# Two-block adaptive attention and feed-forward kernel: transposed queries moved by DMA, another order of the iteration, opening rebuilt

## The chip, the core and the metric

The kernel runs on one core of a Trainium2 chip. A core has TensorE (PE in the profile), VectorE (DVE), ScalarE (ACT), GpSimd (POOL) and SyncE (SP), each with its own instruction queue, which is worked off in order; the engines meet only through semaphores. DMAs are issued from the queue of SP or of ACT. The metric is device time in microseconds (us), the median of the runs.

## The reference

Sixteen sequences of 256 tokens and 256 features. What matters here is the first half, the attention block; the second half (a conditional feed-forward layer "cond2" and a gated feed-forward network "ffn" of width 1024) is not touched by the change.

```python
def _L0_cond_ref(hidden_states, language_ids, W1, b1, W2, b2, gamma, beta):
    w1, w2 = W1[language_ids], W2[language_ids]
    h = relu(einsum('bsh,bha->bsa', hidden_states, w1) + b1[language_ids][:, None, :])
    x = hidden_states + einsum('bsa,bah->bsh', h, w2) + b2[language_ids][:, None, :]
    normed = (x - mean(x)) * rsqrt(var(x) + 1e-5)
    return normed * gamma[language_ids][:, None, :] + beta[language_ids][:, None, :]

def _L0_attn_ref(x, segment_pos, Wq, Wk, Wv, Wf, bf):      # 16 heads of 16, one key and one value head
    q = (x @ Wq.T).reshape(b, t, 16, 16); k = x @ Wk.T; v = x @ Wv.T
    logits = einsum('btnh,bsh->bnts', q, k) * 16 ** -0.5    # causal mask
    probs = softmax(where(mask, logits, -1e30))
    return einsum('bnts,bsh->btnh', probs, v).reshape(b, t, 256) @ Wf.T + bf

x = x + _L0_attn_ref(_L0_cond_ref(x, ...), ...)
x = x + _L0_ffn_ref(_L0_cond2_ref(x, ...), ...)
```

## The kernel before

The attention block is a software pipeline over the 16 sequences. One call of `iteration(b, ...)` on each engine holds four strands at once: the **front** of sequence b + 2 (adapter, layer norm, projections), the **maxima** of sequence b + 1 (all scores, and on DVE their row maxima, in 12 units), the **softmax** of sequence b (scores again with the maximum folded in as extra rows of the product, and exponentials on ACT, in 12 units), and the **tail** of sequence b - 1 (products with the values, division, output projection). Iterations -1 and 0 open the pipeline, B - 2 = 14 and B - 1 = 15 close it, the 13 between them (1 to 13) hold all four strands. There is no scheduler: on each engine the order of the work is the order in which `iteration` calls its helpers.

Scores are computed in float32r (one pass), and keep float32 accuracy by stacking: a column of `q_t` (128 partitions, two heads of 64 rows) has 16 rows of the high part of a query, 16 rows of its low part, 16 rows of the high part again, and two rows for the maximum; `keys` has the matching rows. In the kernel before, the queries are projected with tokens on partitions (`project_queries`, L1200, two halves of 272 columns, with the values in the last 16), DVE splits them into high and low parts in `q_parts` (`queries_of`, L881 to L885), POOL copies the high part once more (`high_again`, L484), PE transposes `q_parts` in 16 blocks of 128x128 per sequence (`queries_transposed`, L1216), and ACT copies the four banks to `q_t` (`queries_out`, L609). Keys are split on DVE (`keys_of`, L869 to L872) and spread over the two heads' row blocks by POOL (`move_keys`, L494); values are copied by POOL (`move_values`, L502). `q_t`, `keys` and `values` have two buffers each.

The maxima are transposed on PE (`maxima_transposed`, L1242), copied by ACT (`maxima_out`, L634) into `m_t`, and moved into the maximum rows of `q_t` by four DMAs of 8 KB on SP's queue (`move_maxima`, L309). The first score product of that sequence waits for them (`scores`, u = 0, L1253). SP's queue holds in each iteration: the front loads of sequence b + 3 (`load_front`, five DMAs), `store_x1`, `load_resid`, then `move_maxima`.

After the pipeline come the cond2 phase (from the end of iteration 15) and the ffn phase, both bound by PE. The weights of the ffn phase are combined by POOL (`combine`), stored to DRAM by a DMA of 1792 KB on ACT's queue (`finish_chunk`, L682) and scanned by ACT (L687); the first such store is issued at the end of iteration 14, between `move_maxima`'s wait and its DMAs.

## Time and profile before

| | us |
|---|---|
| median of 3 runs | 1155.56 (1155.26 to 1156.74) |
| the profiled execution, its own time | 1157.74 |
| its span, first to last instruction | 1156.0 |
| opening, to the first maxima transpose | 42.55 |
| iteration 0 | 18.97 |
| iterations 1 to 13 | 282.37 (steady ones 21.56 each) |
| iteration 14 | 19.12 |
| to the first product with the values of sequence 15 | 20.20 |
| cond2 and ffn phases | 772.79 |

PE is busy 97% of the span, DVE 70%, ACT 51%, POOL 19%. A busy PE in the profile includes the modelled ends of pipelined matmuls, so the cost of a group of matmuls is read from its start to the start of the next group. The stages are cut at the starts of L1242, one per sequence.

### The profile page before, as it was taken

What the parts mean: (1) busy time and instruction counts of PE and PEld (TensorE: products, weight loads), DVE (VectorE), ACT (ScalarE), POOL (GpSimd) and SP (SyncE); (2) the same over time, 40 slices, a digit from 0 to 9 for tenths busy, and PEclk for the clock granted to TensorE, in tenths of its full rate; (3) what the DMA queues carried; (4) which work ended last, traced back from release to release, by engine and by line L of the source; (5) the groups of instructions that cost most, each with busy time, mean ns of one, the idle gap of its engine ahead of it and who ended that gap; (6) DMA issues with size and microseconds to landing.
All of it is one profiled execution on the core that took longest, in us unless ns stands there. A gap on an engine that the chain in (4) does not pass through costs nothing.

```text
span 1156.0 us, 18793 instructions
## 1 busy us (share of the span) xinstructions
PE 1117.5 (97%) x6148; PEld 892.6 (77%) x6178; DVE 804.4 (70%) x1440; ACT 594.7 (51%) x989; POOL 214.6 (19%) x266
## 2 busy tenths in 40 slices
PE   4899999999998999999999999999999999999998
PEld 3567777777775788888888888888888888888886
DVE  2877777776776557756577875778656887568875
ACT  1355655555555634533365654556445565455653
POOL 2233333343345444452000000000000000000000
PEclk9999999999999999999999999999999999999999
DMA  4342122122143456654515443044440444304420
GB/s 122 111 149 60 53 59 63 48 60 63 47 160 124 151 187 202 227 188 150 204 35 164 140 167 115 10 164 146 162 137 0 163 146 163 137 8 145 145 91 37
DMA packets 66765, 135.97 MB, mean 118 GB/s; under 512 B 13793, under 2 KB 28017, under 8 KB 66545
## 3 DMA queue, kind: packets, MB, share of 16 engines
q1 hardware_dynamic: 57696, 114.49, 30.5%
q10 hardware_dynamic: 9024, 20.97, 5.0%
q8 instruction: 18, 0.29, 0.1%
q14 instruction: 27, 0.21, 0.1%
HBM read 107.65 MB, written 30.41 MB: 119 GB/s over the span
## 4 chain that ended last, share of the span: by engine, by line
PE 89%; DVE 6%; SPq 2%; issue 1%; DMA 1%; ACT 1%; POOL 0%; DVEq 0%; POOLq 0%; ACTq 0%
PE bank L1531 35%; PE bank L1493 10%; PE bank L1319 7%; PE bank L1543 5%; PE bank L1469 4%; PE bank L1463 4%; PE bank L1253 4%; PE bank L1234 3%; DVE neg_max L891 2%; PE bank L1274 2%; PE bank L1311 2%; PE bank L1216 2%; PE bank L1200 2%; PE bank L1237 1%; PE bank L1189 1%
## 5 line engine op out<-in xcount | busy, mean ns | idle before, releaser
L1531 PE MATMUL bank<-op_lo,w_ring 128*128 128x512 f32 x896 | 348.6, 389 | 0.0
L1531 PE MATMUL bank<-op_hi,w_ring 128*128 128x512 f32 x896 | 348.6, 389 | 0.0
L1066 DVE TENSOR_TENSOR op_lo<-x_blk,op_hi 128x512 fp32r<-128x512 f32 x288 | 193.8, 684 | 30.4 <-ACT op_hi L764 30.3
L764 ACT ACTIVATE op_hi<-x_blk 128x512 fp32r<-128x512 f32 x288 | 162.8, 620 | 73.6 <-PE bank L1531 69.3
L1531 PEld LDWEIGHTS bank<-op_lo,w_ring 128*128 128x128 f32 x896 | 168.2, 188 | 34.9
L1531 PEld LDWEIGHTS bank<-op_hi,w_ring 128*128 128x128 f32 x896 | 168.2, 188 | 34.9
L891 DVE TENSOR_REDUCE neg_max<-bank 128x2 f32<-128x512 f32 (+1 forms) x192 | 126.0, 685 | 48.0 <-remote 39.7
L617 ACT ACTIVATE p<-bank 128x512 f32<-128x512 f32 x192 | 111.3, 599 | 71.9 <-PE bank L1253 68.2
L788 ACT ACTIVATE x_blk<-x_blk,scales 128x512 f32<-128x512 f32 x96 | 69.3, 722 | 67.0 <-DVE x_blk L1119 28.9
L1493 PE MATMUL bank<-tile_hi,ffn_w 128*128 128x512 f32 x256 | 101.5, 396 | 0.0
L1493 PE MATMUL bank<-tile_lo,ffn_w 128*128 128x512 f32 x256 | 101.5, 396 | 0.0
L1253 PE MATMUL bank<-q_t,keys 128*128 128x512 f32 x192 | 95.5, 515 | 4.8 <-DMA q_t<-m_t 4.2
L1234 PE MATMUL bank<-keys,q_t 128*128 128x256 f32 (+1 forms) x256 | 86.0, 392 | 7.5 <-DVE neg_max L891 6.4
L717 ACT ACTIVATE g_raw<-bank,fc_bias 128x512 f32<-128x512 f32 x64 | 44.0, 689 | 92.2 <-PE bank L1319 77.9
L511 POOL TENSOR_SCALAR_AFFINE_SELECT p<-p 128x512 f32<-128x512 f32 (+1 forms) x96 | 75.8, 789 | 66.8 <-ACT p L617 66.8
L776 ACT ACTIVATE sil<-bank,scales 128x512 f32<-128x512 f32 x64 | 44.0, 689 | 79.7 <-PE bank L1493 79.7
L1074 DVE SCALAR_TENSOR_TENSOR x_blk<-bank,scales,sil 128x512 f32<-128x512 f32 x64 | 48.1, 751 | 52.4 <-PE bank L1493 50.2
L1234 PEld LDWEIGHTS bank<-keys,q_t 128*128 128x128 f32 x256 | 48.1, 191 | 20.2 <-DVE neg_max L891 10.7
L562 POOL TENSOR_TENSOR comb<-comb 128x512 f32<-128x512 f32 x32 | 49.5, 1547 | 56.5 <-DVE g_parts L1032 55.0
L1493 PEld LDWEIGHTS bank<-tile_hi,ffn_w 128*128 128x128 f32 x256 | 48.2, 188 | 11.7
L1493 PEld LDWEIGHTS bank<-tile_lo,ffn_w 128*128 128x128 f32 x256 | 48.2, 188 | 11.7
L1032 DVE TENSOR_TENSOR g_parts<-g_raw,g_parts 128x512 fp32r<-128x512 f32 x64 | 52.1, 814 | 2.2
(124 smaller groups left out, 1850.0 us busy)
## 6 DMA issues: line engine op xcount, KB each, us to landing
w_ring<-hid_scratch SPq DMA_DIRECT2D x112, 512.0 KB, 4.6
hid_scratch<-comb ACTq DMA_DIRECT2D x8, 1792.0 KB, 7.6
comb<-in_hid_d ACTq DMA_DIRECT2D x6, 768.0 KB, 5.1
xt<-in_x_t SPq DMA_DIRECT2D x16, 256.0 KB
xtok<-in_x_tok SPq DMA_DIRECT2D x16, 256.0 KB
resid<-in_x_t SPq DMA_DIRECT2D x16, 256.0 KB, 3.1
x_scratch<-x SPq DMA_DIRECT2D x16, 256.0 KB, 2.6
tile_in<-x_scratch SPq DMA_DIRECT2D x8, 512.0 KB, 4.1
```

Source lines behind the costliest of these rows:

```text
L511: nc.gpsimd.affine_select(out=v, in_=v, compare_op=ALU.is_ge, fill=0.0, base=0, pattern=[[0, v.shape[1]], [1, P]], channel_multiplier=-1). ...
L617: nc.scalar.activation(dst.rearrange("p c t -> p (c t)"), score_bank[par][:, :], ACT.Exp).then_inc(s["exp_done"], 1)
L764: nc.scalar.activation(op_hi[:, o % OP_RING, k], x_blk[:, operand_home(o), k], ACT.Copy).then_inc(s["op_hi"], 1)
L788: nc.scalar.activation(x_blk[:, at[block], m], src, ACT.Gelu, scale=sc[:, KB * row + m:KB * row + m + 1]).then_inc(s[made], 1)
L891: nc.vector.tensor_reduce(neg_max[:, t, first:first + pairs, :].rearrange("p c a -> p (c a)"), max_bank[u % 2][:, :].rearrange("p (c k) -> ...
L1066: nc.vector.tensor_tensor(op_lo[:, o % OP_RING, k], x_blk[:, operand_home(o), k], op_hi[:, o % OP_RING, k].bitcast(F32), ALU.subtract).the ...
L1234: mm(dst[:, 2 * c * seen:2 * (c + 1) * seen].rearrange("p (a k) -> p a k", a=2), q_t[odd][:, first + c, t * P:(t + 1) * P], keys[odd][:, : ...
L1253: mm(score_bank[par][:, :].rearrange("p (c t) -> p c t", c=pairs), keys[odd][:, par, k0:k0 + P], q_t[odd][:, first:first + pairs, q0:T], s ...
L1319: last = mm(bank, w[:, k, cols], v[:, k, :], start=i == 0, stop=i == len(passes) - 1)
L1493: last = mm(bank, w_at(at, k, HID, m), read(v[:, half, k, :]), start=k == 0 and v is yc_hi, stop=k == KD - 1 and v is yc_lo)
L1531: last = mm(banks[first_bank + m][:, :], w, read(v[:, q % OP_RING, k, :]), start=k == 0 and v is op_hi and i not in (P2, P3), stop=k == KB ...
L1543: last = mm(banks[4 + 2 * half + m][:, :], w_at(W3_AT, k, D, m), read(v[:, o % OP_RING, n % KB, :]), start=n == 0 and v is op_hi, stop=n = ...
```

## The change

- **Queries transposed by the projection.** `wqv` and `wk` become `wq` and `wkv`. `project_queries` now computes with the weights as the stationary operand, so that the result comes out with features on partitions and tokens on columns, in one bank; the columns of `wq` are ordered so that partition hd * 8 + pair holds one row of a head. ACT takes the high part (`queries_high`), DVE the low one (`queries_low`). The rows are then brought into `q_t` by six DMAs of 128 KB per sequence: four for the two copies of the high part, on ACT's queue (`move_high`), two for the low part on SP's queue (`move_queries`). `queries_transposed`, `queries_out`, `queries_of` and `high_again` are gone.
- **Keys and values** are projected together. ACT copies the bank to `kv` (`keys_copied`) and writes both row blocks of `keys` (`keys_high`), DVE subtracts for the low rows (`keys_low`), PE transposes `kv` in two blocks (`values_transposed`), DVE copies the values out (`values_of`). `move_keys` and `move_values` on POOL are gone.
- **Three buffers** (`SLOTS = 3`) for `q_t`, `keys` and `values`; the hardware loop holds three iterations.
- **Another order** of the helpers in `iteration` on PE, DVE, ACT, POOL, and of SP's queue: rest of the loads, front loads, `move_queries`, `move_maxima`, then `store_x1`, `load_resid`.
- **Opening**: the loads of sequence 0's adapter weights go on ACT's queue, beside those on SP's; nine matmuls on zeros (`keep_warm`) and a dummy activation (`warm_row`) run before the data is there; iteration -1 has an order of its own: the whole front of sequence 1, then the maxima of sequence 0.
- **End**: `finish_chunk` is cut into `store_chunk` and `check_chunk`; the first store waits until the last maxima have been moved.

The core of the diff:

```diff
+SLOTS = 3
+            def move_queries(n, slot):
+                sp.wait_ge(s["q_low"], n + 1)
+                settle(sp, "sp_settled")
+                for par in range(2):
+                    row = SLOT * par + HD
+                    sp.dma_start(q_t[slot][row:row + HD, :, :].bitcast(F32), q_rest[:, par, :].bitcast(F32)).then_inc(s["q_moved"], 16)
...
-                    load_front(b + 3)
+                    load_rest(b + 3, l)
+                    load_inputs(b + 3, l)
+                    move_queries(b + 2, (step + 2) % SLOTS)
+                    move_maxima(b + 1, (step + 1) % SLOTS)
                     store_x1(b - 1)
                     load_resid(b)
-                    move_maxima(b + 1, 1 - step % 2)
...
+            def queries_high(n):
+                act.wait_ge(s["q_mm"], n + 1)
+                if not is_first(n):
+                    act.wait_ge(s["q_moved"], 96 * n)
+                nc.scalar.activation(q_high[:, :, :], ring[0][:, :].rearrange("p (a t) -> p a t", a=2), ACT.Copy, scale=QSCALE).then_inc(s["q_hi"], 1)
+            def move_high(n, slot):
+                act.wait_ge(s["q_hi"], n + 1)
+                for i in (0, 2):
+                    for par in range(2):
+                        row = SLOT * par + HD * i
+                        act.dma_start(q_t[slot][row:row + HD, :, :].bitcast(F32), q_high[:, par, :].bitcast(F32)).then_inc(s["q_moved"], 16)
+            def keys_copied(n):
+                act.wait_ge(s["kv_mm"], n + 1)
...
+                nc.scalar.activation(kv[:, :], ring[1][:, 0:T], ACT.Copy).then_inc(s["kv_out"], 1)
+            def keys_high(n, slot):
+                act.wait_ge(s["kv_out"], n + 1)
+                for par in range(2):
+                    nc.scalar.activation(keys[slot][:, par, :], kv[:, :], ACT.Identity,
+                                         bias=key_row[:, 2 * par:2 * par + 1], scale=key_row[:, 2 * par + 1:2 * par + 2]).then_inc(s["keys_hi"], 1)
...
+            def project_queries(n, tail):
+                pe.wait_ge(s["norm_t_out"], n + 1)
...
+                for m in range(KD):
+                    for k in range(KD):
+                        last = mm(ring[0][:, m * T:(m + 1) * T], wq[:, k, m * P:(m + 1) * P], norm_t[:, k, :], start=k == 0, stop=k == KD - 1)
+                last.then_inc(s["q_mm"], 1)
...
+            def values_transposed(n):
+                pe.wait_ge(s["kv_out"], n + 1)
+                for t in range(NT):
+                    last = nc.tensor.transpose(ring[1][:, T + t * P:T + (t + 1) * P], kv[:, t * P:(t + 1) * P], ident[:, :])
+                last.then_inc(s["v_t_mm"], 1)
...
             def max_scores(n, slot, u):
...
                 if u == 0:
-                    pe.wait_ge(s["keys_moved"], 2 * (n + 1))
-                    pe.wait_ge(s["qv_out"], NT * (n + 1))
+                    pe.wait_ge(s["q_moved"], 96 * (n + 1))
+                    pe.wait_ge(s["keys_out"], 2 * (n + 1))
...
+                if softmax and not maxima:
+                    act.wait_ge(s["maxima_moved"], 64 * B)
+                    store_chunk(0)
...
+            nc.vector.memset(warm, 0.0).then_inc(s["warm_made"], 1)
+            pe.wait_ge(s["warm_made"], 1)
+            keep_warm(WARM_LOADS)
```

PE at the end of a full iteration and the beginning of the next. Before (`bank<-wqv,norm_t` is the projection of queries and values, `bank<-ident,m` the transpose of the maxima, `bank<-ident,q_parts` that of the queries, `bank<-xt,w1c` the first matmul of the next front):

```order
L1200 MATMUL bank<-wqv,norm_t 128x272 x2
L1311 MATMUL bank<-att_t,wf 128x256 x4
L1250 REGISTER_ALU
L1253 MATMUL bank<-q_t,keys 128x512
L1250 REGISTER_ALU
L1253 MATMUL bank<-q_t,keys 128x512
L1242 MATMUL bank<-ident,m 32x128 x2
L1197 REGISTER_ALU
L1200 MATMUL bank<-wqv,norm_t 128x272 x2
L1206 REGISTER_ALU
L1216 MATMUL bank<-ident,q_parts 128x128 x8
```

And now (`bank<-ident,kv` is the transpose of the values):

```order
L1365 MATMUL bank<-att_t,wf 128x256 x4
L1307 REGISTER_ALU
L1310 MATMUL bank<-q_t,keys 128x512
L1307 REGISTER_ALU
L1310 MATMUL bank<-q_t,keys 128x512
L1299 MATMUL bank<-ident,m 32x128 x2
L1273 MATMUL bank<-ident,kv 128x128 x2
L1307 REGISTER_ALU
L1310 MATMUL bank<-q_t,keys 128x512
L1221 ISA
L1225 REGISTER_ALU
L1227 MATMUL bank<-xt,w1c 128x256 x2
```

The transposes of the queries and the second half of their projection have left this place; the last score product of the sequence now stands behind the transpose of the values, as PE's last work ahead of the next front. The projection of the queries itself now stands earlier, ahead of four maximum units and the projection of the keys.

ACT in the second half of a full iteration. Before (`p<-bank` is an exponential, `att_t<-bank` the transposed attention, `m_t<-bank` the maxima, `q_t<-bank` the transposed queries):

```order
L602 ACTIVATE norm_t<-bank,vec 128x256 x2
L628 ACTIVATE att_t<-bank 128x512
L613 REGISTER_ALU
L617 ACTIVATE p<-bank 128x512
L613 REGISTER_ALU
L617 ACTIVATE p<-bank 128x512
L613 REGISTER_ALU
L617 ACTIVATE p<-bank 128x512
L613 REGISTER_ALU
L617 ACTIVATE p<-bank 128x512
L631 REGISTER_ALU
L633 REGISTER_ALU
```

And now:

```order
L631 ACTIVATE p<-bank 128x512
L603 ISA
L604 ACTIVATE q_high<-bank 128x512
L612 DMA q_t<-q_high 16x8x256 x4
L617 REGISTER_ALU
L618 ACTIVATE kv<-bank 128x256
L623 ACTIVATE keys<-kv,key_row 128x256 x2
L627 REGISTER_ALU
L631 ACTIVATE p<-bank 128x512
L647 ISA
L648 ACTIVATE m_t<-bank 32x256
```

Between the exponentials 8 and 9 of a sequence stand now the high parts, four DMA issues, the copy of keys and values and the two writes of `keys`.

## Rows read from the trace of the kernel before

**Rows 1.** Busy time by stage: us, then each engine's busy time; PEclk is the granted clock
```profile
0.00:42.55 42.55, 23.90 (x88) 16.54 (x89) 20.04 (x47) 6.43 (x11) 7.09 (x17) 0.96 0.39 115
61.52:343.89 282.37, 275.53 (x2132) 205.21 (x2159) 205.81 (x481) 156.62 (x298) 107.65 (x159) 1.00 0.25 76
343.89:363.01 19.12, 17.73 (x145) 12.69 (x146) 14.04 (x28) 10.96 (x21) 13.26 (x16) 1.00 0.24 72
363.01:383.21 20.20, 16.02 (x111) 10.59 (x109) 9.08 (x13) 11.58 (x19) 8.04 (x8) 0.83 0.44 146
```
**Rows 2.** Timeline of PE, one steady iteration: start us, us, engine, line, what
```profile
192.85 1.04 PE L1216 MATMUL bank<-ident,q_parts 128*128 128x128 f32 x8
193.72 1.03 PE L1166 MATMUL bank<-xt,w1c 128*128 128x256 f32 x4
...
196.48 0.64 PE L1274 MATMUL bank<-p,values 128*32 128x256 f32 x8
...
199.22 0.50 PE L1253 MATMUL bank<-q_t,keys 128*128 128x512 f32 x1
...
208.31 1.03 PE L1189 MATMUL bank<-norm_t,wk 128*128 128x256 f32 x4
208.99 0.58 PE L1253 MATMUL bank<-q_t,keys 128*128 128x512 f32 x1
209.41 0.40 PE L1234 MATMUL bank<-keys,q_t 128*128 128x512 f32 x1
...
210.13 1.08 PE L1200 MATMUL bank<-wqv,norm_t 128*128 128x272 f32 x4
211.05 1.94 PE L1311 MATMUL bank<-att_t,wf 128*128 128x256 f32 x8
212.63 0.82 PE L1253 MATMUL bank<-q_t,keys 128*128 128x512 f32 x2
213.29 0.38 PE L1242 MATMUL bank<-ident,m 128*32 128x128 f32 x2
213.51 1.08 PE L1200 MATMUL bank<-wqv,norm_t 128*128 128x272 f32 x4
```
**Rows 3.** Timeline of ACT, the same iteration
```profile
199.85 2.39 ACT L617 ACTIVATE p<-bank 128x512 f32<-128x512 f32 x4
...
207.12 1.02 ACT L602 ACTIVATE norm_t<-bank,vec 128x256 f32<-128x256 f32 x2 [1.07 <-PE bank L1183]
...
214.22 0.36 ACT L634 ACTIVATE m_t<-bank 32x256 fp32r<-32x256 f32 x1
```
**Rows 4.** Timeline of SP's queue, the same iteration: the issues of the maxima's DMAs
```profile
194.33 2.87 SPq L309 DMA_DIRECT2D q_t<-m_t  x4
```
**Rows 5.** The tile `m_t`: ns min/median/max of one issue
```profile
L309 SPq DMA_DIRECT2D q_t<-m_t x64: 625/660/1374, 43.4 to 369.4; - x64
```
**Rows 6.** Timeline of ACT's queue: one issue of the store of the combined weights
```profile
398.60 0.38 ACTq L682 DMA_DIRECT2D hid_scratch<-comb  x1
```
**Rows 7.** The chain that ended last, iterations 14 and 15: start us, us, what
```profile
349.01 1.94 DMA q_t<-m_t
351.00 0.50 PE bank L1253
...
369.41 3.17 DMA q_t<-m_t
372.63 0.51 PE bank L1253
```
**Rows 8.** DMA issues of the page: queue, count, KB each, us from issue to landing
```profile
resid<-in_x_t SPq DMA_DIRECT2D x16, 256.0 KB, 3.1
```
**Rows 9.** Timeline of the opening
```profile
7.96 2.05 PE L1166 MATMUL bank<-xt,w1c 128*128 128x256 f32 x4 [7.96 <-DMA vec<-in_cond_vec]
...
10.09 1.28 ACT L597 ACT_TABLE_LOAD   x1 [10.09 <-PE bank L1166]
...
48.53 0.50 PE L1253 MATMUL bank<-q_t,keys 128*128 128x512 f32 x1 [0.67 <-DMA q_t<-m_t]
```

More of the change, by code:

```diff
@@ L207, in build @@
         ident = sb("ident", [P, P], F32, one)
-        values = [sb(f"values{i}", [P, NT, 32], F32, one) for i in range(2)]
+        values = [sb(f"values{i}", [P, NT, 32], F32, one) for i in range(SLOTS)]
         pv = sb("pv", [P, 4, T], F32, one)
@@ L939, in iteration @@
                 if maxima:
+                    maximum(b + 1, 0)
+                    maximum(b + 1, 1)
+                if front:
+                    normalise(b + 2)
+                if maxima:
                     maximum(b + 1, 2)
-                    maximum(b + 1, 3)
                 if tail:
@@ L949, in iteration @@
                     maximum(b + 1, 5)
+                    maximum(b + 1, 6)
+                    maximum(b + 1, 7)
+                    maximum(b + 1, 8)
+                    maximum(b + 1, 9)
                 if front:
[L951 to L956 removed]
+                    queries_low(b + 2)
                 if maxima:
```

541 lines of the change are left out of this document (282 added, 259 removed).

## The prediction

> **What bounds the kernel now.** I read the busy time by stage first. In the thirteen full iterations PE is busy 275.53 of 282.37 us, an idle time of 6.84 us or 0.53 per iteration, with the clock at its full level, while DVE is busy 73%, ACT 55% and POOL 38% [rows 1]. So PE sets the pace there, and work that leaves PE is time, as long as nothing else comes late in its place. Next the timeline of PE over one steady iteration, from one transpose of the maxima (L1242) to the next: 21.56 us; the mean of the thirteen is 21.72, the first and the last being longer [rows 1, 2]. Then ACT and SP's queue for the same stretch, because the change gives ACT new duties [rows 3, 4]. Last, the ends: between 363.01 and 383.21 the granted clock is 0.83 on average and PE is idle for 4.2 us [rows 1], and the chain there runs through the maxima's DMA, 3.17 us, where iteration 14 had 1.94 [rows 7].
>
> **PE's own work.** Taken from start to start. Removed: two groups of eight query transposes. The one shown lasts from 192.85 to 193.72, 0.87, so 1.74 for both. The projection of the queries was two groups of 0.92 (210.13 to 211.05); its new shape, four matmuls of 256 columns by two blocks, is that of the output projection, 1.58 (211.05 to 212.63), so 0.26 less. Added: two transposes of the values, priced like the two of the maxima, 0.22 (213.29 to 213.51) [rows 2]. Sum -1.74 - 0.26 + 0.22 = -1.78. Without any idle time the iteration would be 21.56 - 1.78 - 0.53 = 19.25. Waits shorter than the modelled tail of a matmul don't show as idle, so up to half a us more may go: floor 18.7 to 19.25.
>
> **ACT's four DMA issues.** This is the term that costs. After the projection of the queries ends (call it T) ACT must do, in order: the high parts, 0.13 after T and 0.60 long like an exponential (2.39 / 4); four issues; the copy of keys and values, 0.36 as for the maxima; two writes of `keys`, 1.02 as for the two of L602; exponential 9, 0.60 [rows 3]. The issue of an SBUF-to-SBUF DMA whose two sides cut the rows differently is in the trace only on SP, four in 2.87 [rows 4], median 0.66, from 0.63 to 1.37 each [rows 5]; the nearest on ACT's own queue is a store, 0.38 [rows 6]. I take 2.87, since shape and spaces are the same. With 0.05 for each of three semaphores: 0.13 + 0.60 + 2.87 + 0.36 + 1.02 + 0.60 + 0.15 = 5.73, plus the last score product, which waits for exponential 9, 0.33: the next iteration can start at T + 6.06. PE's own way there is four maximum units of 0.36 (209.41 to 210.13 holds two), the keys 0.68, the output projection 1.58, three score products of 0.33 (212.63 to 213.29 holds two) and two transposes of 0.22 [rows 2]: 5.13. So ACT is late by 0.93, and PE waits that long ahead of its last score product. Floor plus 0.93 gives 19.6 to 20.2; I take **19.8** per iteration: 13 x 19.8 = 257.4 against 282.37, **-25.0 us**.
>
> **What could be late next.** The queries: the last high part's issue starts at T + 2.95, and with 1.94 [rows 7] to 3.1 us [rows 8] to land they are there by T + 6.1. PE needs them at the first maximum unit, some 4.7 us into the next iteration (T + 10.8): 4.7 us to spare. The low parts, issued from SP after one DVE operation, are no later. The maxima: ACT copies them behind exponential 9, until T + 6.1; three issues of 0.72 and 1.94 for the last bring T + 10.3. PE reaches the first score product 5.50 after the start of the front (193.72 to 199.22 [rows 2]), less one maximum unit that is now behind it, so at T + 11.1: 0.8 to spare. SP no longer puts a store and a load ahead of these DMAs. The front's loads are issued by T, 6 us before they are wanted. DVE loses two passes of the query split and POOL the copies; neither was bound.
>
> **Opening.** For it: the adapter's weights come from a second queue, three issues earlier (about 1.5 us); the table load, 1.28, leaves the path; the warm-up matmuls let the first adapter matmuls run at the full clock: the first group takes 2.05 for what costs 1.03 later [rows 2, 9], so about 1 us each for two groups. Together the norm of sequence 0 is some 4.9 us earlier. Against it: twice, for sequences 0 and 1, ACT's four issues (2.87) and the copy stand ahead of the values' transpose, and on PE that transpose stands ahead of the next adapter matmul and of the third maximum unit; behind it ten maximum units follow, each paced by DVE, where before the maxima began ahead of the front's middle. I get the first score product, 48.53 before [rows 9], at 50.3, and lose little more in iteration 0: **+1.5 us**, between -4 and +5, as the clock stays up or not. The Trainium skill, TensorE: Matmul & The Clock Gate, Part 1, says that the half rate is the default, that activity releases it and that idleness brings it back. By that rule the gap between the adapter and the norm can undo the warm-up, the worse half of this range; the trace agrees that the first group ran at half the speed of the later ones.
>
> **The end.** In iteration 14 the first score product came 7.1 us after the transpose of the maxima (343.89 to 351.00 [rows 1, 7]); now 0.93 + 0.36 + 4.1 = 5.8 at most, -1.3, and eight transposes go, -0.9. In iteration 15 the store of 1792 KB no longer runs beside the last maxima, and a store and a load no longer precede them on SP: the wait of about 3 us goes (369.41 to 372.63 [rows 7]). Without it the clock should not fall (0.83 in this stage, 1.00 in its neighbours [rows 1]), and from the first score product to the products with the values, 10.6 us (372.63 to 383.21), should take about twelve exponentials and one copy, 8: -2.6. Together **-8 us**, between -9.5 and -5. The phases behind have no edit that reaches them.
>
> **Sum.** -25.0 + 1.5 - 8.0 = -31.5. The profiled execution took 1157.74 (span 1156.0), which becomes 1126.2; it lay 2.2 above the median of the runs, so on the median, 1155.56, I forecast **1124.0 us**. Its own range: 19.2 to 20.4 per iteration with the ends' bounds, 1113 to 1135.
>
> **Rivals.**
> - *Cheap issues.* If ACT issues as on its own store, 0.38 each [rows 6], ACT's way is 1.35 shorter, less than PE's 5.13, and PE waits for nothing: 19.0 per iteration, -35.4; the opening gains 2.7 of the same: -44.6, **1111 us**. For: it is ACT's own queue. Against: the shape is another. 0.14.
> - *More hand-offs than I counted.* The iteration becomes shorter than its chains DVE-PE-ACT allow here and there, each wait short: 20.8, -12.0, with the ends -18.5: **1137 us**. The 0.53 of idle time with a longer iteration speaks for some. 0.12.
> - *Late queries.* All six transfers write 16 partitions each. The data part of 256 KB over 128 partitions is 3.1 - 1.94 = 1.16, so 0.58 for 128 KB. Were each four times as slow and the four one after another, 9.3, they would land at T + 12.1, 1.3 too late: 21.1 per iteration, -8.1, and the opening 3 worse: -11.6, **1144 us**. The Trainium skill, SBUF — State Buffer, section "Door 1: The DMA port swizzle", says that DMA bandwidth depends on how many of the 16 ports the partitions reach, and by its formula 16 neighbouring partitions reach four; no row of this case shows that. 0.10.
> - *Slower: dear issues.* If one issue on ACT takes what the slowest on SP took, 1.37 [rows 5], ACT is 2.6 us later still in each iteration: 22.4, +8.9, the opening 5.2 worse, the end as above: +7.6, **1163 us**. It decides from 31.5 / 60 = 0.53 above 0.72, so from 1.25 us per issue (52 issues in the loop, 8 in the opening). For: 16 rows to 128 partitions is more than the 8 KB on SP. Against: the median of 0.66. 0.09.
> - *It comes to nothing*, two of these in part: within 0.2% of before, 0.03.
>
> **How the numbers follow.** Likeliest 0.52 (1124), cheap issues 0.14, hand-offs 0.12, late queries 0.10: faster 0.88. Same 0.03. Slower 0.09. The bound of 0.2% (2.3 us) is about what a measurement of this kernel can tell from no change. The range takes in all but the last two and the outer parts of the first two: 1106 to 1146.
>
> **What would show it.** In the profile after: no idle time of PE but one near 0.9 us ahead of the last score product of each sequence, ended by ACT's exponential; ACT's queue with four issues in 2.9; the period between transposes of the maxima 19.8; the clock at 1.00 through iteration 15 and no wait there for `q_t<-m_t`; the first score product near 50. If ACT's issues take over 1.2 us, or PE's first maximum unit waits for the moved queries, the forecast is wrong; if PE's idle time has gone and the period is 19 or less, ACT was cheaper than I took it.

## The result, and the profile after

The changed kernel takes **1161.16 us** (median of 20 runs, 1157.3 to 1167.22) beside 1156.67 for the kernel before (20 runs, 1155.26 to 1161.41): ratio 1.003, 95% interval 1.0018 to 1.0041. It is slower by a little, where 1124.0 was forecast. (Here and below the ratio and its interval are the recorded estimate; the quotient of the two medians printed beside it can differ by up to 0.002.) Its profiled execution has a span of 1160.3 us, 4.3 above that of before.

The steady loop did become shorter, and about as much as forecast. Nearly all of it was given back elsewhere. The first view to read is therefore the busy time by stage, with the cuts at the transposes of the maxima as in [rows 1]. The columns are the stretch, its length, the busy time of PE, PE's weight loads, DVE, ACT and POOL with their instruction counts, the granted clock, the DMA engines' busy share and GB/s. Of the changed kernel:

```profile
0.00:56.24 56.24, 33.66 (x88) 20.12 (x89) 19.82 (x46) 8.62 (x16) 7.67 (x18) 0.80 0.47 102
56.24:75.20 18.96, 17.24 (x64) 11.64 (x66) 13.11 (x25) 7.68 (x15) 3.77 (x5) 0.77 0.23 58
75.20:96.00 20.80, 19.76 (x152) 14.42 (x154) 13.91 (x32) 12.56 (x25) 5.54 (x7) 1.00 0.91 275
96.00:126.23 30.23, 21.48 (x152) 15.23 (x152) 14.88 (x34) 12.02 (x25) 5.44 (x7) 0.83 0.47 101
126.23:348.33 222.10, 216.28 (x1663) 158.34 (x1673) 163.31 (x364) 130.98 (x252) 62.59 (x79) 1.00 0.52 113
348.33:370.47 22.14, 18.23 (x128) 11.78 (x128) 14.43 (x27) 10.16 (x20) 9.86 (x9) 0.85 0.40 83
370.47:388.47 18.00, 14.68 (x112) 9.29 (x111) 10.90 (x14) 12.69 (x20) 9.92 (x10) 1.00 0.48 163
```

And of the kernel before, two stages that [rows 1] holds only within its steady stretch (iterations 1 and 2):

```profile
61.52:83.63 22.11, 21.47 (x165) 15.75 (x167) 15.46 (x37) 11.19 (x22) 8.16 (x13) 1.00 0.53 175
83.63:105.50 21.87, 21.22 (x166) 15.79 (x167) 15.80 (x38) 12.21 (x24) 8.13 (x13) 1.00 0.20 57
```

| stage | before | after | difference |
|---|---|---|---|
| opening, to the first transpose of the maxima | 42.55 | 56.24 | +13.7 |
| iteration 0 | 18.97 | 18.96 | 0.0 |
| iteration 1 | 22.11 | 20.80 | -1.3 |
| iteration 2 | 21.87 | 30.23 | +8.4 |
| iterations 3 to 13 | 238.39 | 222.10 | -16.3 |
| iteration 14 | 19.12 | 22.14 | +3.0 |
| iteration 15, to its first product with the values | 20.20 | 18.00 | -2.2 |
| all behind it | 772.8 | 771.8 | -1.0 |
| span | 1156.0 | 1160.3 | +4.3 |

Each column is one execution. Where experiments below leave a stage's code as it is, their executions show how much it moves by itself: the changed kernel's opening took 56.24 here and 55.33 in e5, its iteration 1 20.80 here and 22.34 and 22.41 in e3 and e5, its iteration 2 between 24.2 and 30.2 (e5, e3, e4, e2). The eleven iterations stay within 0.15 us (e1, e2, e5, e8), but for e3 with 223.48, and the part behind within 0.05.

**The steady iteration.** PE of the changed kernel, from the query projection to the next iteration, to be laid beside [rows 2] (start us, us, engine, line, what, and in brackets an idle time and what ended it):

```profile
200.82 1.89 PE L1257 MATMUL bank<-norm_t,wq 128*128 128x256 f32 x8
...
207.10 0.38 PE L1299 MATMUL bank<-ident,m 128*32 128x128 f32 x2
...
208.18 0.50 PE L1310 MATMUL bank<-q_t,keys 128*128 128x512 f32 x1 [0.48 <-ACT p L631]
```

and ACT for the same stretch, beside [rows 3]:

```profile
202.83 0.60 ACT L604 ACTIVATE q_high<-bank 128x512 fp32r<-128x512 f32 x1 [1.08 <-PE bank L1257]
203.46 2.55 ACTq L612 DMA_DIRECT2D q_t<-q_high  x4
206.13 0.38 ACT L618 ACTIVATE kv<-bank 128x256 f32<-128x256 f32 x1 [2.70 <-issue]
206.55 1.09 ACT L623 ACTIVATE keys<-kv,key_row 128x256 fp32r<-128x256 f32 x2
207.55 0.57 ACT L631 ACTIVATE p<-bank 128x512 f32<-128x512 f32 x1
```

The chain is there in the order forecast: high parts, four issues in 2.55 us, the copy of keys and values held up behind them for 2.70, the two writes of `keys`, the exponential, and PE waiting 0.48 for it. The period is 20.05 us, with every third at 20.46; the mean of the eleven is 222.10 / 11 = 20.19, against 238.39 / 11 = 21.67. Of the 16.3 us, 1.3 are iteration 13: before waits 1.31 there for DVE's norm, at 337.08, and takes 22.82 for it where its other ones take 21.56.

**The opening.** PE's timeline of the changed kernel:

```profile
1.53 4.02 PE L1490 MATMUL bank<-att 128*128 128x512 bf16 x9 [1.53 <-DVE att L1058]
9.05 2.04 PE L1227 MATMUL bank<-xt,w1c 128*128 128x256 f32 x4 [3.50 <-DMA vec<-in_cond_vec]
...
17.68 1.09 PE L1246 MATMUL bank<-ident,norm 128*128 128x128 f32 x4 [3.89 <-DVE norm L908]
...
27.53 0.69 PE L1273 MATMUL bank<-ident,kv 128*128 128x128 f32 x2 [2.75 <-ACT kv L618]
28.01 1.91 PE L1227 MATMUL bank<-xt,w1c 128*128 128x256 f32 x4
...
36.28 1.12 PE L1246 MATMUL bank<-ident,norm 128*128 128x128 f32 x4 [3.72 <-DVE norm L908]
38.51 3.78 PE L1257 MATMUL bank<-norm_t,wq 128*128 128x256 f32 x8 [1.11 <-ACT norm_t L596]
41.73 1.87 PE L1291 MATMUL bank<-keys,q_t 128*128 128x256 f32 x4
```

and the same places of the kernel before:

```profile
17.89 1.09 PE L1183 MATMUL bank<-ident,norm 128*128 128x128 f32 x4 [3.91 <-DVE norm L859]
...
27.83 0.58 PE L1234 MATMUL bank<-keys,q_t 128*128 128x256 f32 x2
```

Up to 28 us the kernels are level: the norm of sequence 0 is transposed at 17.68 and 17.89. Then before starts its maximum units at 27.83, and runs the front of sequence 1 between them. The changed kernel runs sequence 1's front alone, with nothing to fill its gaps, and starts its maximum units at 41.73: 13.9 us later, which is the whole of the +13.7. One window over it shows the price twice, in idle time and in the clock (0.50 is the lower of the two levels, 1.2 GHz):

```profile
28.00:41.73 13.73, 8.34 (x23) 5.51 (x21) 5.60 (x14) 2.09 (x5) 0.70 (x1) 0.50 0.45 77
```

**Iteration 2.** One wait on PE, and SP's queue ahead of it:

```profile
105.85 2.07 PE L1227 MATMUL bank<-xt,w1c 128*128 128x256 f32 x4 [8.29 <-DMA w2c<-in_cond_w]
```
```profile
80.02 0.44 SPq L413 DMA_DIRECT2D comb<-in_hid_d  x1
...
82.79 0.60 SPq L337 DMA_DIRECT2D ffn_scratch<-in_ffn_d  x1
...
91.25 0.58 SPq L294 DMA_DIRECT2D w1c<-in_cond_w  x1
92.02 0.47 SPq L295 DMA_DIRECT2D w2c<-in_cond_w  x1
```

`w2c` is 65 KB. PE is ready for it at 97.56, 5.5 us after its issue, and gets it at 105.85, 13.8 us after. Ahead of it are 2 MB of combining loads and the ffn store (3 MB, the size of the load that reads it back), issued from 80.02 to 83.39. Iteration 1, in which they start, has a DMA share of 0.91, where the eleven iterations behind have 0.52. In the kernel before, the loads and the store stand apart: SP issues the four loads from 38.65 to 40.50, in the opening, and the store at 65.29:

```profile
65.29 0.60 SPq L317 DMA_DIRECT2D ffn_scratch<-in_ffn_d  x1
```

The change moved only the four loads, from the opening to directly ahead of the store. The store stands behind `move_maxima(1, 1)` in both kernels, and by itself there it made PE wait for no front load in iteration 2 of the kernel before, where iteration 1 had a DMA share of 0.53.

**Iteration 14.** What PE waits for, and POOL's queue, in which the causal mask (L520) stands behind a combining step (L561):

```profile
350.84 0.49 PE L1310 MATMUL bank<-q_t,keys 128*128 128x512 f32 x1 [1.17 <-ACT p L631]
...
355.46 1.08 PE L1329 MATMUL bank<-p,values 128*32 128x256 f32 x8 [1.81 <-POOL p L520]
```
```profile
351.68 1.70 POOL L561 TENSOR_TENSOR comb<-comb 128x512 f32<-128x512 f32 x1
353.33 2.07 POOL L520 TENSOR_SCALAR_AFFINE_SELECT p<-p 128x1024 f32<-128x1024 f32 x1
```

### The profile page after: what moved, and what is told of

The parts are those of the page before. It is cut to its first block, busy times and chain, and to the rows that moved or that the text cites. A ratio compares the mean times of both kernels' runs of the same rounds, so it can differ in the third digit from the quotient of the medians.

```text
span 1160.3 us, 17988 instructions
## 1 busy us (share of the span) xinstructions
PE 1108.4 (96%) x5947; PEld 876.8 (76%) x5963; DVE 788.9 (68%) x1377; ACT 593.1 (51%) x990; POOL 175.8 (15%) x192
## 4 chain that ended last, share of the span: by engine, by line
PE 87%; ACTq 4%; ACT 3%; issue 2%; DVE 2%; DMA 2%; POOL 1%; SPq 0%; DVEq 0%; POOLq 0%
PE bank L1605 35%; PE bank L1567 10%; PE bank L1373 7%; PE bank L1617 5%; PE bank L1543 4%; PE bank L1537 4%; PE bank L1310 4%; ACTq L612 3%; PE bank L1291 3%; PE bank L1329 3%; PE bank L1257 3%; PE bank L1237 2%; PE bank L1227 2%; PE bank L1294 2%; DMA w2c<-in_cond_w 1%
## 5 line engine op out<-in xcount | busy, mean ns | idle before, releaser
L631 ACT ACTIVATE p<-bank 128x512 f32<-128x512 f32 x192 | 110.2, 593 | 29.5 <-PE bank L1310 23.8
L520 POOL TENSOR_SCALAR_AFFINE_SELECT p<-p 128x512 f32<-128x512 f32 (+1 forms) x96 | 77.7, 810 | 168.8 <-ACT p L631 168.7
L1310 PE MATMUL bank<-q_t,keys 128*128 128x512 f32 x192 | 89.4, 506 | 9.1 <-ACT p L631 9.0
L1291 PE MATMUL bank<-keys,q_t 128*128 128x256 f32 (+1 forms) x256 | 92.3, 415 | 2.2 <-DVE neg_max L935 2.1
L561 POOL TENSOR_TENSOR comb<-comb 128x512 f32<-128x512 f32 x32 | 50.2, 1567 | 56.5 <-DVE g_parts L1093 55.0
L1294 PE MATMUL bank<-mask,ident_b 128*128 128x256 bf16 (+1 forms) x176 | 56.3, 320 | 0.0
```

The costliest lines, as they stand in the source:

```text
L520: nc.gpsimd.affine_select(out=v, in_=v, compare_op=ALU.is_ge, fill=0.0, base=0, pattern=[[0, v.shape[1]], [1, P]], channel_multiplier=-1). ...
L631: nc.scalar.activation(dst.rearrange("p c t -> p (c t)"), score_bank[par][:, :], ACT.Exp).then_inc(s["exp_done"], 1)
L1291: mm(dst[:, 2 * c * seen:2 * (c + 1) * seen].rearrange("p (a k) -> p a k", a=2), q_t[slot][:, first + c, t * P:(t + 1) * P], keys[slot][:, ...
L1294: mm(diag, ident_b[:, :], mask[:, 0:2 * pairs, :], start=False, stop=True).then_inc(s["max_mm"], 1)
L1310: mm(score_bank[par][:, :].rearrange("p (c t) -> p c t", c=pairs), keys[slot][:, par, k0:k0 + P], q_t[slot][:, first:first + pairs, q0:T], ...
```

## The experiments

Each was timed beside the kernel before on the same chip, in one of three groups: before took 1158.14 us for e1 to e4, 1157.8 for e5 to e8, 1157.7 for e9 and e10. Across groups the ratios are compared; the changed kernel's is 1.003. In the diffs a minus is a line of the kernel named, a plus one of the experiment. Stage lengths come from each one's profiled execution.

**e1, the bulk transfers in the opening.** The four loads go back to the place that they have in the kernel before, and the store goes into the opening as well, where before doesn't have it. (The later expectations call both "as before" or "at their old place"; that is right of the loads alone.) On the changed kernel:

```diff
             move_queries(0, 0)
+            store_ffn()
             load_front(2)
+            (the four loads of comb[0], comb[1])
             sp.wait_ge(s["const_made"], 3)
...
             move_maxima(1, 1)
-            (the four loads of comb[0], comb[1])
-            store_ffn()
```

> The changed kernel with one thing moved on SP's queue: the 3 MB copy of the ffn weights and the 2 MB of loads for the combining are issued in the opening, behind the first sequence's query moves, and no longer at 80 us, ahead of iteration 2's loads. Theory 1 (these transfers hold up the front loads of iteration 2, on which PE waits 8.3 us): the stage from the third to the fourth transpose of the maxima falls from 30.2 to about 20.3, and the whole by 8 to 10 us against the changed kernel, ratio to before 0.996. Rival (the moved queries' own traffic, 768 KB per sequence, is what delays the loads): the wait stays or moves to another iteration, and the whole stays within 2 us of the changed kernel.

Measured: 1152.31 us, ratio 0.9934 (0.9909 to 0.9959). Iteration 2 takes 20.08 instead of 30.23, with no DMA wait of PE, while the opening stays at 56.20:

```profile
97.47:117.55 20.08, 19.61 (x152) 14.40 (x152) 14.88 (x34) 12.03 (x25) 5.45 (x7) 1.00 0.51 98
```

Iteration 1 takes 22.39 where it took 20.80, so the two together fall by 8.6, from 51.03 to 42.47. So the 8.4 us that iteration 2 had over before are the doing of where the 5 MB are issued. The edit moves both parts; a run with the loads alone at their old place wasn't made.

**e2, the opening in the order of the other iterations.** On the changed kernel, in ACT's, DVE's and PE's `iteration`:

```diff
-                if not softmax:
-                    (an order of its own for the opening's iteration -1)
-                    return
```

> The changed kernel without the special order of iteration -1: it runs in the order of the other iterations, with the maximum units of sequence 0 between the steps of sequence 1's front. Theory 1 (the opening is long because twelve maximum units and their DVE steps stand behind the whole front of sequence 1): the first transpose of the maxima comes at 46 to 48 us and no longer at 56.2, the whole falls by 8 to 10 us. Rival (the opening is long because TensorE runs at half its clock and ACT issues four DMAs ahead of the keys, whatever the order): the first transpose stays above 54.

Measured: 1152.14 us, ratio 0.9948 (0.9929 to 0.9966). The opening takes 45.84 instead of 56.24, and iteration 2 keeps its wait (7.64 for `w2c`, 29.97 us long):

```profile
0.00:45.84 45.84, 29.61 (x86) 17.86 (x88) 18.63 (x41) 7.79 (x15) 7.68 (x18) 0.89 0.48 116
```

Of the opening's 13.7 us, 10.4 are this order. The other 3.3 are not taken apart. In this execution the first maximum unit starts at 32.37, where before has 27.83; ahead of it PE waits 2.27 us for ACT's copy of keys and values, which stands behind the four issues, and 1.07 us for `q_t<-q_high`. There is also a granted clock of 0.89 where before has 0.96 [rows 1]. Another wait, 2.31 for `q_t<-q_rest` at 51.32, falls into iteration 0.

**e3, no warm-up.** `WARM_LOADS, WARM_NORM = 9, 14` becomes `0, 14`: the nine matmuls on zeros ahead of the first adapter product are left out.

> The changed kernel without the nine warm-up matmuls. In its trace the first adapter group took 2.04 us after them, as long as 2.05 before, so theory 1 says they buy nothing: the whole within 1 us of the changed kernel, first transpose of the maxima at 56. Rival (they shorten the opening by letting the later groups reach the full clock): 2 us or more slower than the changed kernel.

Measured: 1161.47 us, ratio 1.0025 (1.0011 to 1.0038), which is the changed kernel's. The opening takes 54.55 where it took 56.24: the warm-up gains nothing here. The first adapter product takes 2.04 behind it, as the 2.05 without a warm-up in [rows 9]; in the loop it takes 1.03 [rows 2].

Three other executions with the same warm-up show what became of it. In e5 the granted clock is 1.00 from 5.20 to 8.60 and 0.50 from 8.60 to 25.60; in e7 it falls at 8.4, in e1 at 9.1. So there the clock did rise, just as the nine matmuls ended (in e5 the ninth took 0.51 us where the eight others took 0.61 to 0.63), and it had fallen again when the first product started, at 8.76, 9.42 and 9.51, since PE had nothing to do until the adapter's data landed. In the changed kernel's execution, in e3's and in the others the clock's record only begins between 23.8 and 24.7 us. Ahead of its first entry the views print 1.00, also where products take 2.04; so the 0.80 of the opening in the first view is too high.

**e4, all transfers of queries issued by SyncE.** They are six a sequence, four high and two low (the later expectations' "eight" is a slip). On the changed kernel:

```diff
-            (ACT) move_high(n, slot): wait for q_hi, four dma_start of q_high
             (SP) move_queries(n, slot):
+                sp.wait_ge(s["q_hi"], n + 1)
+                (four dma_start of q_high)
                 sp.wait_ge(s["q_low"], n + 1)
```

> The changed kernel with all six moves of the queries issued from SP's queue, none from ACT's. Theory 1 (the four issues, 2.5 us, keep ACT from the exponential on which PE's last score product waits): ACT's gap ahead of the copy of the keys goes, PE's wait of 0.45 ahead of the last score product goes, the steady period falls from 20.05 to 19.5 or less, the whole by 5 to 8 us against the changed kernel; the opening gets shorter by some 2 us twice. Rival (two queues are needed, six issues in a row on one queue land too late for the first maximum unit, or delay the maxima's own DMAs): PE waits at the first maximum unit or the first score product, the whole the same or slower.

Measured: 1147.26 us, ratio 0.99 (0.9881 to 0.9919), 1.3% below the changed kernel.

```profile
0.00:52.66 52.66, 31.39 (x89) 18.72 (x90) 19.74 (x46) 8.62 (x16) 7.68 (x18) 0.87 0.49 109
121.60:338.87 217.27, 216.46 (x1663) 158.38 (x1673) 163.38 (x364) 133.82 (x254) 62.09 (x79) 1.00 0.55 116
338.87:356.52 17.65, 15.69 (x129) 10.73 (x129) 15.13 (x27) 8.77 (x17) 8.69 (x9) 1.00 0.49 100
```

The eleven iterations take 217.27 instead of 222.10, and PE is idle for 0.8 us of them instead of 5.8: ACT's issues cost 4.83 / 11 = 0.44 per iteration, the wait of 0.48. They cost another 3.6 in this order of the opening (2.7 against the 55.33 of e5) and 4.5 in iteration 14, where the clock now stays up. The whole gained 13.9 us where 5 to 8 had been expected: the expectation had no term for iteration 14. The transfers land as fast from SP, 4.0 us against 4.1 for the high parts in the loop: no wait for `q_t` there.

**e5, the masks first.** On the changed kernel, in POOL's `iteration`:

```diff
+                if softmax:
+                    causal(b, 5)
                 if last_front:
                     combine(0, 2)
                 elif last_maxima:
                     combine(1, 1)
-                if softmax:
-                    causal(b, 5)
```

> The changed kernel, with one step of GpSimd's order moved: the last causal mask of an iteration stands ahead of the combining of the scores, which only iterations 14 and 15 have. Theory 1: iteration 14 of the changed kernel takes 22.1 us where before took 19.1, and 1.8 of the 3 us are TensorE's wait for that last mask, which stands behind a combine of 1.7 us; the same wait in iteration 15 is 1.5 us. Then iteration 14 takes 20.3 to 20.8, the wait of the value products for the mask is gone from both, and the whole is 2 to 3.5 us shorter than the changed kernel (about 1158.5 to 1159). Rival: ScalarE, with its four issues, sets iteration 14; the value products then wait as long for the exponentials instead of the mask, iteration 14 stays at 22 and the whole at 1161.

Measured: 1155.76 us, ratio 0.9983 (0.9967 to 0.9999): 0.5% below the changed kernel. Iteration 14 is 18.32 us long, a gain of 3.8 where the wait aimed at was 1.81, and the clock is at its full level where it was 0.85; the wait of 1.17 for the exponential is still there. Iteration 15 gives 1.0 more (17.00 to its first product with the values), the wait of 1.52 for its last mask being gone:

```profile
342.89:361.21 18.32, 15.87 (x129) 10.68 (x128) 14.32 (x27) 10.00 (x20) 9.45 (x9) 1.00 0.45 97
```

e4 left the mask behind the combine, with 1.52 of wait for it, and had 17.65 all the same. So the +3.0 needed both: the exponentials late behind ACT's issues, and the mask behind a combine. Either edit alone takes it away. In this profiled execution, the fastest of its ten, iteration 2 also took 24.21, with 2.31 of wait for `w2c` instead of 8.29. The code at that place is the same in five kernels, and the waits are 8.29 (changed kernel), 7.64 (e2), 7.23 (e4), 2.50 (e3) and 2.31 (e5): the size of this loss varies from execution to execution, and 8.4 is one draw of it. The store lands at 99.6 in the changed kernel's execution and at 95.9 and 96.0 in e3's and e5's.

**e6, the kernel before with its first store of combined weights late.** On the kernel before, ACT's part for the last iterations:

```diff
+                if softmax and not maxima:
+                    act.wait_ge(s["maxima_moved"], 64 * B)
+                    store_chunk(0)
                 if softmax:
                     for u in range(0, 4):
...
                 if maxima and not front:
-                    finish_chunk(0)
+                    check_chunk(0)
```

(`finish_chunk` is parted into its store and the rest. The expectation gives that store 256 KB; the page has it at 1792.)

> The kernel before, with one part of the change's end: the first store of combined scores (256 KB) is issued by ScalarE after the last maxima have been moved, not ahead of them. Theory 1: that store was in the way of the transfers of sequence 14's and 15's maxima, for which TensorE waited 1.94 and 3.17 us; with the store out of the way iterations 14 and 15 lose 3 to 5 us, and the whole comes to 1152 to 1154 where before is 1156.7. Rival: those waits were the transfers' own time at that place and not the store's doing; the waits stay above 1.5 us each and the whole stays within 1 us of before.

Measured: 1152.81 us, ratio 0.9953 (0.9933 to 0.9973). From the last transpose of the maxima to the first product with sequence 15's values it takes 15.09 where before took 20.20, and the score product waits for no DMA but 0.46 for ACT:

```profile
362.40:377.49 15.09, 13.57 (x112) 8.96 (x110) 9.03 (x13) 11.61 (x19) 8.05 (x8) 1.00 0.60 194
```
```profile
370.16 0.98 PE L1260 MATMUL bank<-q_t,keys 128*128 128x512 f32 x2 [0.46 <-ACT p L617]
```

The 5.1 us of this stage are the 5.0 of the median. Iteration 14 stays as it was, 19.11 with its own wait for `q_t<-m_t`; the expectation's 1.94 there is the transfer's landing time in the chain, of which PE was idle for 0.48 only.

**e8, e1 and e2 together.**

> The changed kernel with the store of the ffn and the first combining loads back at their old place, and no order of its own for the opening's first iteration; ScalarE keeps its four issues. Theory 1: the two alone gave -8.9 and -9.0 us against the changed kernel, in stages that don't meet: together 1143 (1141 to 1146), the opening at 46 and iteration 2 at 20. Rival: the early stores and loads run into the transfers of an opening that is 10 us shorter: iteration 2 or the opening keeps 4 us or more, and the whole is 1147 to 1152. The difference between this kernel and the one with all transfers on SyncE's queue is what ScalarE's four issues cost over the whole kernel: 13 to 14 us by theory 1.

Measured: 1148.07 us, ratio 0.9903 (0.9876 to 0.9929). The rival's number holds: the two don't add up. The place is another than it named: the opening is 45.78 and iteration 2 20.06, but now iteration 0 takes 26.11, with a wait of 8.36 for `q_t<-q_rest` at 57.31. In e1 alone the same burst had an opening 10 us longer to pass in; that this is why it hurt nobody there is argued, not shown.

**e7, e8 with e4 and e5 as well.**

> The changed kernel with four parts set otherwise at once: all eight transfers of transposed queries issued by SyncE, none by ScalarE; the store of the ffn and the first combining loads issued ahead of the front's loads, as before; no order of its own for the opening's first iteration; the last mask ahead of the combine. Theory 1: the three costs are in different stages (opening -10, iteration 2 -8 to -9, ScalarE's issues -14 with iteration 14 among them) and add up: opening 43 to 46 us, iteration 2 at 19.7, later iterations at 19.6, the whole near 1129 (1126 to 1133), 2.4% below before. Rival: they meet in one queue. With eight issues of 0.7 us a sequence on SyncE behind it, the combining loads and the stores collide with the moved loads, and iteration 2 keeps 3 us or more of its wait; or the opening, where SyncE now has all the work, gives back less than 5 us: the whole is then above 1136.

Measured: 1137.43 us, ratio 0.9808 (0.9783 to 0.9834), above the 1136 at which the rival was to hold. The parts that the rival named gave back what they should (opening 46.77, iteration 2 20.52); the loss is in iteration 0, 26.46 us long. Against e8 it is 10.6 us faster, where 13 to 14 were expected for ACT's issues, and 3.6 of these are iteration 14, which e7's mask accounts for in part. In the opening the issues cost nothing here: 46.77 without them on ACT, 45.78 with them in e8. Two waits for moved queries, one in the opening and one in iteration 0:

```profile
33.35 0.79 PE L1258 MATMUL bank<-keys,q_t 128*128 128x256 f32 x2 [4.23 <-DMA q_t<-q_rest]
59.03 0.80 PE L1258 MATMUL bank<-keys,q_t 128*128 128x256 f32 x2 [9.09 <-DMA q_t<-q_rest]
```

SP's queue just ahead of the second: four combining loads, 2 MB, and directly behind them the moves of 128 KB on which iteration 0 depends.

```profile
41.39 0.42 SPq L414 DMA_DIRECT2D comb<-in_hid_d  x1
...
43.51 2.71 SPq L321 DMA_DIRECT2D q_t<-q_high  x4
```

The kernel before issues the same four loads at about that place (38.65), and its iteration 0 has no queries that go by DMA. With queries that do, the same place is a bad one.

**e9, e7 with the 5 MB parted.**

```diff
             (SP: the last load of the constants)
+            store_ffn()
             load_front(1)
             sp.wait_ge(s["const_made"], 1)
             move_queries(0, 0)
-            store_ffn()
             load_front(2)
-            (the loads of comb[0], comb[1])
             sp.wait_ge(s["const_made"], 3)
             move_queries(1, 1)
             move_maxima(0, 0)
+            (the loads of comb[0])
             load_front(3)
             move_queries(2, 2)
             move_maxima(1, 1)
+            (the loads of comb[1])
```

> The kernel with all eight transfers on SyncE and four parts set otherwise, once more, with the 5 MB of the ffn store and the first combining loads parted: the store (3 MB) goes out in the opening, ahead of sequence 1's front loads, and one chunk of combining loads (1 MB) behind each of the first two moves of maxima. Theory 1 (where a burst is issued decides whom it holds up): the two waits for q_t<-q_rest of that kernel, 4.2 us in the opening and 9.1 us in iteration 0, were the burst's doing, since the store was issued 1 us and the combining loads 1 to 3 us around those moves; without it iteration 0 takes 19 to 20 where it took 26.5, no w2c wait comes back in iteration 2, and the whole is 8 to 12 us shorter: 1128 (1125 to 1131). Rival: the moves of 128 KB are late for another reason, the six issues in a row on SyncE, and the waits stay in good part: the opening at 46 and iteration 0 at 24 or more, the whole above 1133.

Measured: **1131.38 us, ratio 0.976 (0.9736 to 0.9784)**, faster than both kernels. The profiled execution took 1135.31, the slowest of the four. Iteration 0 takes 19.58 instead of 26.46, iteration 2 20.17:

```profile
45.73:65.31 19.58, 15.33 (x66) 10.45 (x67) 14.14 (x29) 9.34 (x18) 3.90 (x6) 0.91 0.62 131
...
85.67:105.84 20.17, 19.62 (x152) 14.39 (x152) 14.84 (x34) 12.14 (x24) 5.42 (x7) 1.00 0.49 98
105.84:323.64 217.80, 216.38 (x1663) 158.34 (x1672) 163.28 (x364) 133.64 (x254) 61.91 (x79) 1.00 0.56 115
```

The gain over e7 is 6 us of the 8 to 12 expected; the whole is just above the range of 1125 to 1131. The wait in the opening stayed, though the store, issued at 8.23, had landed at 21.8, so it was not the burst's doing, and that part goes to the rival, the six issues in a row on SP (24.39 to 28.29, the low parts last). Two more are left in the execution shown:

```profile
32.90 0.79 PE L1259 MATMUL bank<-keys,q_t 128*128 128x256 f32 x2 [4.82 <-DMA q_t<-q_rest]
51.34 0.80 PE L1259 MATMUL bank<-keys,q_t 128*128 128x256 f32 x2 [2.44 <-DMA q_t<-q_rest]
330.98 0.80 PE L1259 MATMUL bank<-keys,q_t 128*128 128x256 f32 x2 [2.74 <-DMA q_t<-q_rest]
```

**e10, e9 with the change's two queues.** The high parts are issued by ACT again.

> The same with the changed kernel's two queues: ScalarE issues the four high moves, SyncE the low ones. Theory 1: the opening and iterations 0 to 2 as with all on SyncE or 1 to 2 us longer, the steady iteration at 20.05 to 20.15 where it is 19.6 to 19.7, iteration 14 near 18.3 (the mask is ahead of the combine): the four issues on ScalarE cost 0.45 us in each of 13 iterations and 1 to 3 us in the opening, 7 to 9 us in all: 1136 (1133 to 1139). Rival: high moves that leave earlier by another queue repay that in the opening, and the two kernels are within 4 us.

Measured: 1139.86 us, ratio 0.9844 (0.9818 to 0.9869), 8.5 us above e9 and inside the 7 to 9 us expected for the price of ACT's issues (the whole is just above its own range of 1133 to 1139):

```profile
108.56:330.92 222.36, 216.28 (x1662) 158.35 (x1672) 163.39 (x364) 131.39 (x253) 62.49 (x79) 1.00 0.52 113
```

The Trainium skill, DMA: Bandwidth & Descriptors, section "Issuing engines are not separate DMA queues", says that issuing from several engines saves only issue time on the sequencer, usually small beside the DMA. The pair agrees that the second queue makes nothing land sooner: in the eleven iterations the high parts land in 4.1 us from either engine. But the issue time is not small where the engine has work behind it, 2.55 us of ACT per sequence. SP issues as fast and computes nothing, so there it holds up only its own queue.

## Why the prediction was wrong

**The steady iteration: right in mechanism, 0.25 too short in size for the period, 0.4 for the mean.** Forecast 19.8, measured 20.05 and 20.19 in the mean. ACT's way was worked out with 2.87 for the issues where 2.55 was measured, so the wait is 0.48 and not 0.93. PE's own work fell less than forecast, from 275.53 / 13 = 21.19 to 216.28 / 11 = 19.66, by 1.53 and not 1.78, and little of the half a us of hidden short waits came free: 20.05 less the wait is 19.57, where the 19.8 had 18.87 in it. So one error made the forecast 0.45 too long and the other 0.7 too short. The turn of the hardware loop, 0.4 us in every third iteration, was in no term. For the thirteen iterations at the measured 20.19 the term would have been -19.9 instead of -25.0. "Cheap issues" and "dear issues" fall: an issue costs 0.62 in the median on ACT, beside 0.66 on SP [rows 5]. "More hand-offs" falls too: the period is not 20.8, and the one wait is where it was forecast.

**The opening: the step that failed first.** Forecast +1.5 (-4 to +5), measured +13.7. Three parts of it went wrong.
- The norm of sequence 0 was to come 4.9 us earlier (its three parts add up to 4.8) and came 0.2 earlier. The loads on the second queue landed at 9.05, later than 7.96 [rows 9]; the matmuls behind the warm-up took 2.04 still, because the higher clock, where the record shows it, was gone again by then (e3). Only the table load left the path, and DVE's part behind it didn't move: 3.89 of wait against 3.91.
- The sentence "ten maximum units follow, each paced by DVE, where before the maxima began ahead of the front's middle" named the mechanism and gave it no price. It is the price: sequence 1's front, 13.7 us on a PE with nothing in its gaps and the clock at 0.50, stood beside the maximum units before and stands ahead of them now. I had the two start times in the order of the changed instructions and never set them on a time line. e2 shows 10.4 us of it.
- The rest, 3.3, is open. In the changed order ACT's issues are 3.6 of the opening by e4; in e2's order they are not, since there the opening takes 45.78 with them on ACT (e8) and 46.77 with all on SP (e7), and 46.98 (e10) against 45.73 (e9) with the store out of the way. The forecast had them in its +1.5, at 2.87 for each of two sequences.

**What could be late next: the transfers were priced as if alone.** "The front's loads are issued by T, 6 us before they are wanted" is right for the steady loop, where the last is issued at 203.05 and wanted at 208.85. It says nothing of iteration 2, where 5 MB in one burst stood in front of them: 2 MB that the change had moved from the opening to 80 us, and the 3 MB store directly behind. I read of SP's queue only that a store and a load left the way of the maxima, not where the bulk went. That is 8.4 us with no term in the sum (2.3 to 8.3 of wait, as it falls); e1 takes it away. The rival "late queries" looked at the width of the transfers, in the steady loop; there they land in 4.1 us (high) and 5.1 (low) and are never waited for. The queries are late only where a bulk transfer or six issues in a row stand ahead (e7, e8, e9).

**The end.** Forecast -8, measured +3.0 - 2.2 = +0.8. The part of iteration 15 was right in cause: without the store there is no wait for `q_t<-m_t` there and the clock stays at 1.00, and e6 shows 5.1 of the forecast 5.8 us in the kernel before. In the changed kernel only 2.2 of it arrives, because a wait of 1.52 for the last mask, where before has 0.56, takes part of its place. e5 shows 1.0 us of it; that the rest, 17.00 against e6's 15.09, is the exponentials coming later is argued, not shown. The forecast's own sum was off too: 0.93 + 0.36 + 4.1 is 5.4 and not 5.8, and of the landing time of 1.94 that it took from the chain PE had waited only 0.48. Iteration 14 was forecast at -2.2 and lost 3.0: the masks' place on POOL, behind a combine, was in no step, and the exponentials behind ACT's issues are late there by 1.17 us where the steady loop has 0.48. e4 and e5 show that the two together make it.

**The sum by measured terms**: opening +13.7, iterations 0 to 2 +7.1, iterations 3 to 13 -16.3, iteration 14 +3.0, iteration 15 -2.2, the rest -1.0: +4.3. The -1.0 of the rest, which no edit was to reach, is no chance: it is 771.8 in all ten executions that have the change and 772.8 in both that don't. Its cause is open. The chance of slower stood at 0.09, for a mechanism (dear issues) that wasn't there; the stages that made it slower, 25 us of losses against 21 of gains, were bounded to 5 or not named at all. (The forecast's own range, 1113 to 1135, isn't what its bounds add up to either: 1109 to 1138.) The range of 1106 to 1146 had the loop's unknowns in it and not those of the iterations around it.

**Open.** Whether a warm-up that reached up to the first product would gain anything: nine matmuls ended 3.5 us too early, and no longer one was run. Why the first loads, some of them issued from ACT's queue, land 1.1 us later than before (PE's first product starts at 8.50 to 9.51 in the ten executions of the change, at 7.96 and 7.85 without it). What holds the moved queries at 330.98 in e9, in one profiled execution; the 3 MB of ffn weights are read back from 310.6 on, and taking them elsewhere wasn't tried. And the 4.82 us in e9's opening, which e10, with two queues, hasn't got: there ACT's copy is late by 2.69 instead, and the opening is longer, 46.98 against 45.73. Issuing from both in the opening and from SP in the loop wasn't run.

## What to carry to other kernels

An engine that issues a DMA is held for each of them (0.62 us here), so issues belong on the queue of an engine that has nothing behind them (1.3% of the whole, e4); ask what stands behind the issue before asking which queue is free. When a change makes a tile travel by DMA, a bulk transfer that hurt nobody can hold it up (e7, e8): list what is in flight at each hand-off, the opening's and the end's above all, and part a burst rather than move it. And a steady loop's gain is the easy half of a forecast: put the first three and the last two iterations on a time line of their own before giving the ends a range.

## What the runs showed of the hardware

- Issuing an SBUF-to-SBUF DMA of 128 KB from 128 partitions into 16 takes ACT 0.55 to 2.19 us, median 0.62, and SP 0.59 to 0.68 in e4's eleven iterations, median 0.61 (one of 3.03 ahead of them, while the 5 MB were in flight); there it lands 4.1 us after its issue from ACT and 4.0 from SP, and six a sequence at a DMA share of 0.52 to 0.56 hold nobody up in the eleven iterations, but for one wait of 1.39 us for `w2c` in e3.
- A move of the same size, a low part, landed after up to 12.4 us with bulk transfers beside it (e8), and after 5.1 in the loop; a load of 65 KB issued 9 us behind 5 MB held PE up by 2.3 to 8.3 us with the same code in five executions.
- A wait can cost more than its length: in iteration 14 one of 1.81 and one of 1.17 us came with a granted clock of 0.85, and without the longer one the stage was 3.8 us shorter (e5), at 1.00. In the opening a stretch with PE busy 8.34 of 13.73 us was granted 0.50 throughout. The Trainium skill, TensorE: Matmul & The Clock Gate, Part 1, says that activity releases the higher rate and idleness takes it back. These two stages agree, and so does the warm-up where the clock's record covers it: 4.0 us of matmuls on zeros brought the clock to 1.00, and it was back at 0.50 before the next product, at half speed (2.04 us), started 3.3 to 4.1 us after the last of them (e1, e5, e7).
